# Fetching the experts' rows earlier, and the last two additions of a mixture-of-experts block in other pieces, on one Trainium2 core

## The chip, the cores and the metric

The kernel runs on one core of one Trainium2 chip. The metric is the device time of one launch in microseconds. The kernel before took 1689.24 us, the median of three runs (1687.09 to 1690.79).

## The reference

Four blocks run one after the other on x of 1024 tokens by 256 channels, all in float32: a gated delta rule attention, a perceptron, an attention with 4 heads and a mixture of experts. Only the last is touched here. Cut to what matters:

```python
xf = layernorm(x)
x_ = w_norm * (xf * rsqrt(mean(xf * xf) + EPS))
probs = softmax(x_ @ w_router)                    # 32 experts
w_topk, sel = top_k(probs, 4)
buf[e, place] = x_[token]                         # up to 128 rows for each expert
g = einsum('ech,ehf->ecf', buf, w_gate)           # F = 176
u = einsum('ech,ehf->ecf', buf, w_up)
y = einsum('ecf,efh->ech', silu(g) * u, w_down)
out = zeros.at[token].add(y * weight)
sh = sigmoid(x_ @ w_shared_gate) * (silu(x_ @ sw_gate) * (x_ @ sw_up) @ sw_down)
return x + xf + out + sh
```

## The kernel before

The program is a row of blocks. At the end of a block all engines meet at a barrier, and within one each engine goes through its own list in order and waits on semaphores. The last part has three blocks: a layer norm, `route_and_share`, and `experts`.

`route_and_share` finds each token's four experts, and GpSimd writes each token's row (289 numbers: 256 channels, 32 weights, the token's number) to its places in the DRAM tensor `expert_rows` (called `buf` in the code) with 32 indirect DMAs (L1657; semaphore `s_scat`). Meanwhile TensorE computes the shared expert (L1555, L1568), and VectorE adds that to x (L1645), which is the last thing in the block.

`experts` goes through the 32 experts one by one. For expert e, SP loads its 128 rows into one of six tiles `be` (L1700) and its down weights into one of four tiles `wd` (L1705). TensorE transposes the rows (`flip`, L1748), VectorE copies the result to `bT` (L1797), TensorE makes gate and up (`hidden`, L1756), ScalarE and VectorE make `hh` (L1843, L1803), TensorE transposes it (`flip_hidden`, L1764), ScalarE copies it (L1849), TensorE multiplies by `wd` (`output`, L1773), VectorE computes the rows' destinations (`places`, L1809 and L1811) and weighs the output into `ys` (`y_out`, L1815), and GpSimd adds `ys` to a sum in DRAM by an indirect DMA that accumulates (L1737). This last step is called the scatter below. There are two such sums, `expert_sum0` for the even experts and `expert_sum1` for the odd ones. A scatter waits until the one before it into the same sum has landed (`s_summed`), and `places(e)` waits for the landing of scatter e-4, since `place` and `ys` have four buffers.

TensorE's list is software pipelined. What is called iteration i below is one turn of this loop:

```python
            for e in range(E + 1):
                if e + 2 < E:
                    flip(e + 2)
                if e + 1 < E:
                    hidden(e + 1)
                if e < E:
                    flip_hidden(e)
                if e >= 1:
                    output(e - 1)
```

SP's list alternates rows and weights for the same expert. Weights of e wait for output e-4 (`s_yb`). So the rows of e, which stand behind the weights of e-1, cannot leave before output e-5 is done, at the end of iteration e-4, and `flip(e)` is the first thing in iteration e-2.

At the end SP waits for both sums, loads each in two halves into `part` (L1719), VectorE adds the four pieces to x (L1835), and SP stores x in two halves (L1724).

## Time and profile before

| | |
|---|---|
| median of 3 runs | 1689.24 us |
| the profiled execution: its own time | 1689.97 us |
| the profiled execution: its span | 1687.5 us |
| route_and_share, from the first product to the last addition | about 1478 to 1556 us |
| experts, from its first load to the last scatter's landing | 1556.6 to 1674.3 us |
| last loads, additions and stores | 1674.3 to 1687.1 us |

The times of the trace count from the start of its span. "PE" is TensorE's matmul side and "PEld" its weight loads, "DVE" is VectorE, "ACT" ScalarE, "POOL" GpSimd, "SPq" an instruction on SP's queue. A row "PE psum_banks L1748 <- DMA moe_be" is idle time of PE that a landing ended.

### The profile page before, as it was taken

How to read it: one execution, taken by the hardware profiler on the slowest of the kernel's cores; microseconds unless marked ns; L12 is line 12 of the kernel's file. 1: busy time of each engine (PE TensorE's matmuls, PEld its weight loads, DVE VectorE, ACT ScalarE, POOL GpSimd, SP SyncE). 2: the span in 40 equal slices, each digit the busy share in tenths (PEclk: the TensorE clock that was granted, in tenths of full speed). 3: DMA queues.
4: the chain of work that ended last, by engine and by line, in shares of the span. 5: the costliest groups of instructions: out<-in, count | busy, mean ns of one | idle time of the engine just before them, and what ended most of it. 6: DMA issues, size and time to landing. Idle time of an engine off the chain costs nothing. (4 is left out here: it accounts for less than half of the span.)

```text
span 1687.5 us, 26280 instructions
## 1 busy us (share of the span) xinstructions
PE 1424.7 (84%) x9464; PEld 1006.2 (60%) x9464; DVE 1058.4 (63%) x2172; ACT 768.4 (46%) x1796; POOL 722.6 (43%) x1181
## 2 busy tenths in 40 slices
PE   1555989999999999999999999988777888699874
PEld 1333667676777676777767767776535455455553
DVE  2534777877878787778787877865322355541443
ACT  0232655656556556565565565664220355110110
POOL 0065374382563653734735637430000288234443
PEclk9977889999999999999999999999888899889997
DMA  8111111111111111111111111010081000112666
GB/s 203 47 29 42 30 33 36 36 33 37 27 40 35 33 36 36 39 36 24 37 36 32 42 30 38 24 20 13 7 327 32 1 1 1 56 46 76 135 136 136
DMA packets 127039, 86.70 MB, mean 51 GB/s; under 512 B 92290, under 2 KB 112982, under 8 KB 126144
## 3 DMA queue, kind: packets, MB, share of 16 engines
q1 hardware_dynamic: 120768, 76.50, 17.1%
q0 software_dynamic: 6144, 8.53, 3.0%
q8 instruction: 76, 1.25, 0.3%
q14 instruction: 51, 0.42, 0.1%
HBM read 61.65 MB, written 23.76 MB: 51 GB/s over the span
## 5 line engine op out<-in xcount | busy, mean ns | idle before, releaser
L614 PE MATMUL psum_banks<-main_hT,heads_w_in 128*128 128x512 f32 x512 | 261.9, 645 | 11.9 <-DMA heads_w_in<-in_w_in 8.1
L939 DVE SCALAR_TENSOR_TENSOR heads_y<-psum_banks,gdn_conv_w,heads_y 128x1021 f32<-128x1021 f32 (+2 forms) x192 | 245.1, 1278 | 37.2 <-ACT heads_y L809 35.2
L1118 POOL TENSOR_TENSOR heads_XT<-heads_XT,heads_tmp 128x126 f32<-128x126 f32 (+22 forms) x496 | 211.8, 427 | 38.8
L1108 POOL TENSOR_TENSOR heads_A<-heads_A,heads_cb 128x1024 f32<-128x1024 f32 x16 | 37.7, 2355 | 397.5 <-DVE heads_nd_t L992 381.0
L1115 POOL TENSOR_TENSOR heads_tmp<-heads_XT,heads_A 128x126 f32<-128x126 f32 (+22 forms) x496 | 180.9, 365 | 38.9
L614 PEld LDWEIGHTS psum_banks<-main_hT,heads_w_in 128*128 128x128 f32 x512 | 102.1, 207 | 108.0 <-issue 92.9
L1445 POOL TENSOR_SCALAR attn_prob<-attn_prob,attn_rtotal 128x1024 f32<-128x1024 f32 x32 | 90.7, 2846 | 149.4 <-DVE attn_rtotal L1412 149.4
L746 PE MATMUL psum_banks<-heads_w_o,heads_ogT 128*128 128x256 f32 x512 | 121.1, 386 | 2.9 <-ACT heads_ogT L875 1.0
L715 PE MATMUL psum_banks<-heads_w_z,main_hT 128*128 128x256 f32 x512 | 123.5, 384 | 0.0
L809 ACT ACTIVATE heads_y<-psum_banks,gdn_conv_w 128x1024 f32<-128x1024 f32 x64 | 71.3, 1115 | 102.8 <-PE psum_banks L614 100.8
L827 ACT ACTIVATE heads_O<-psum_banks,gdn_coef 128x128 f32<-128x128 f32 x224 | 69.8, 363 | 86.2 <-PE psum_banks L645 84.0
L834 ACT ACTIVATE heads_Dt<-heads_Dl,gdn_coef 128x128 f32<-128x128 f32 x224 | 77.3, 393 | 66.9 <-DVE heads_Dl L952 66.5
L746 PEld LDWEIGHTS psum_banks<-heads_w_o,heads_ogT 128*128 128x128 f32 x512 | 95.1, 193 | 19.9 <-issue 8.5
L715 PEld LDWEIGHTS psum_banks<-heads_w_z,main_hT 128*128 128x128 f32 x512 | 93.1, 192 | 11.2
L947 DVE SCALAR_TENSOR_TENSOR heads_X<-psum_banks,gdn_coef,heads_v_s 128x128 f32<-128x128 f32 x224 | 67.8, 344 | 50.9 <-PE psum_banks L643 50.8
L652 PE MATMUL psum_banks<-heads_X,heads_Uf 128*128 128x128 f32 x448 | 75.5, 292 | 21.5 <-DVE heads_X L947 21.5
L652 PEld LDWEIGHTS psum_banks<-heads_X,heads_Uf 128*128 128x128 f32 x448 | 62.5, 193 | 52.1 <-issue 31.2
L952 DVE COPY heads_Dl<-psum_banks 128x256 f32<-128x256 f32 x128 | 53.8, 420 | 63.3 <-PE psum_banks L652 62.8
L845 ACT ACTIVATE heads_junk<-heads_og 128x128 f32<-128x128 f32 x256 | 78.0, 305 | 33.9 <-DVE heads_og L978 29.5
L658 PE MATMUL psum_banks<-heads_Dl,heads_At 128*128 128x128 f32 x512 | 86.6, 293 | 3.8 <-DVE heads_Dl L952 3.8
L1737 POOL DMA_INDIRECT expert_sum<-moe_ys,moe_place x32 | 49.6, 1549 | 80.8 <-DVE moe_ys L1815 76.9
L1132 POOL TENSOR_TENSOR heads_rs<-heads_var,gdn_minus_half 128x16 f32<-128x16 f32 x16 | 46.4, 2901 | 86.5 <-DVE heads_var L1063 86.5
(249 smaller groups left out, 3115.8 us busy)
## 6 DMA issues: line engine op xcount, KB each, us to landing
main_w_gu<-in_w_gu SPq DMA_DIRECT2D x4, 2816.0 KB, 24.7
heads_w_in<-in_w_in SPq DMA_DIRECT2D x16, 512.0 KB, 3.5
heads_A<-kk_blocks SPq DMA_DIRECT2D x64, 128.0 KB, 2.7
moe_wd<-in_w_down SPq DMA_DIRECT2D x32, 176.0 KB
expert_rows<-main_zeros SPq DMA_DIRECT2D x1, 4624.0 KB, 29.1
moe_be<-expert_rows SPq DMA_DIRECT2D x32, 144.5 KB, 3.3
heads_w_z<-in_w_z SPq DMA_DIRECT2D x16, 256.0 KB, 2.7
heads_w_o<-in_w_o SPq DMA_DIRECT2D x16, 256.0 KB, 2.6
```

The costliest lines, as they stand in the source:

```text
L614: ins = pe.matmul(out[:, half * 512:(half + 1) * 512], w_in[:, kd_, j * P:(j + 1) * P], hT[:, kd_, half * 512:(half + 1) * 512], start=kd_ ...
L652: ins = pe.matmul(bank_a[:, e], Uf[old][:, e * C + c], rhs, start=True, stop=True)
L658: ins = pe.matmul(bank_b[:, e], At[old][:, c * HD + e], Dl[:, e], start=True, stop=True)
L715: ins = pe.matmul(flat(bank[b][:, 2 * j:2 * j + 2]), hT[:, k, c * P:(c + 1) * P], w_z[:, k], start=k == 0, stop=k == KD - 1)
L746: ins = pe.matmul(flat(bank[b][:, 2 * j:2 * j + 2]), ogT[:, c * HD + e], w_o[:, e], start=e == 0, stop=e == HD - 1)
L809: act.activation(y[j][:], out, ACT.Copy, scale=conv_w[:, head, j, 3:4]).then_inc(pair_base.sem, 1)
L834: ins = act.activation(Dt[:, e], Dl[:, e], ACT.Copy, scale=coef[:, TAIL, h - 1, i:i + 1])
L845: act.activation(junk[:], og[(h - 1) % 2][:, c * HD + e], ACT.Square, accum_out=ms[:, c * HD + e:c * HD + e + 1]).then_inc(sq_ready.sem, 1)
L939: dve.scalar_tensor_tensor(y[j][:, shift:T], src[:, 0:T - shift], conv_w[:, head, j, t:t + 1], y[j][:, shift:T], ALU.mult, ALU.add).then_i ...
L1115: pool.tensor_tensor(tmp[:, 0:n, 0:m], bc_last(XT[:, 0:n, j], m), bc_mid(A0[:, j, j + 1:BLK], n), ALU.mult).then_inc(solve_step.sem, 1)
L1118: pool.tensor_tensor(XT[:, 0:n, j + 1:BLK], XT[:, 0:n, j + 1:BLK], tmp[:, 0:n, 0:m], ALU.add).then_inc(solve_step.sem, 1)
L1445: pool.tensor_scalar(prob[p % 2][s][:], prob[p % 2][s][:], rtotal[:, n:n + 1], None, ALU.mult).then_inc(s_norm, 1)
```

## The change

SP loads the first four `wd` tiles at the start of `route_and_share` and the first six `be` tiles in that same block, once all 32 scatters into `expert_rows` have landed. For this `be`, `wd` and their semaphores are made outside `experts`. In `experts`, SP's turn e now loads the rows of e+2 (after `y_out` and `places` of e-4) and then the weights of e (after output e-4). At the end, `expert_sum0` is waited for and loaded by itself in two halves, then `expert_sum1` in four quarters; VectorE makes two additions of 1024 and four of 512 elements a partition, and SP stores four quarters. No computation is left out.

```diff
+QUARTERS = 4
...
+        def load_rows(sp, e):
+            sp.dma_start(be[e % UB][:], buf[e * CAP:(e + 1) * CAP]).then_inc(s_be[e % UB], 16)
+
+        def load_down(sp, e):
+            sp.dma_start(wd[e % UN][:], d["w_down"][e]).then_inc(s_wd[e % UN], 16)
...
     with nc.Block() as block:
+        @block.sync
+        def _(sp):
+            for e in range(UN):
+                load_down(sp, e)
+            sp.wait_ge(s_scat, 16 * N)
+            for e in range(UB):
+                load_rows(sp, e)
...
-            def load_rows(e):
-                if e >= UB:
-                    sp.wait_ge(s_ys, e - UB + 1)
-                    sp.wait_ge(s_place, e - UB + 1)
-                sp.dma_start(be[e % UB][:], buf[e * CAP:(e + 1) * CAP]).then_inc(s_be[e % UB], 16)
-
-            def load_down(e):
-                if e >= UN:
-                    sp.wait_ge(s_yb, e - UN + 1)
-                sp.dma_start(wd[e % UN][:], d["w_down"][e]).then_inc(s_wd[e % UN], 16)
-
-            for e in range(UN):
-                load_rows(e)
-            for e in range(UN):
-                load_down(e)
             for e in range(UN, E):
-                load_rows(e)
-                load_down(e)
-            for i in range(SUMS):
-                sp.wait_ge(s_summed[i], 16 * (E // SUMS))
+                ahead = e + UB - UN
+                if ahead < E:
+                    sp.wait_ge(s_ys, ahead - UB + 1)
+                    sp.wait_ge(s_place, ahead - UB + 1)
+                    load_rows(sp, ahead)
+                sp.wait_ge(s_yb, e - UN + 1)
+                load_down(sp, e)
+            sp.wait_ge(s_summed[0], 16 * (E // SUMS))
             for half in range(2):
-                for i in range(SUMS):
-                    rows = sums[i][half * HALFT * P:(half + 1) * HALFT * P].rearrange("(t p) n -> p t n", p=P)
-                    sp.dma_start(part[i][:, half * HALFT:(half + 1) * HALFT], rows).then_inc(s_part[2 * i + half], 16)
+                rows = sums[0][half * HALFT * P:(half + 1) * HALFT * P].rearrange("(t p) n -> p t n", p=P)
+                sp.dma_start(part[0][:, half * HALFT:(half + 1) * HALFT], rows).then_inc(s_part[half], 16)
+            sp.wait_ge(s_summed[1], 16 * (E // SUMS))
+            for i in range(QUARTERS):
+                rows = sums[1][i * QT * P:(i + 1) * QT * P].rearrange("(t p) n -> p t n", p=P)
+                sp.dma_start(part[1][:, i * QT:(i + 1) * QT], rows).then_inc(s_part[2 + i], 16)
             o = out.rearrange("a (t p) n -> p (a t) n", p=P)
-            for half in range(2):
-                sp.wait_ge(s_add, SUMS * (half + 1))
-                mine = slice(half * HALFT, (half + 1) * HALFT)
+            for i in range(QUARTERS):
+                sp.wait_ge(s_add, 2 + i + 1)
+                mine = slice(i * QT, (i + 1) * QT)
                 sp.dma_start(o[:, mine], x[:, mine]).then_inc(s_out, 16)
...
             for half in range(2):
-                mine = x[:, half * HALFT:(half + 1) * HALFT]
-                for i in range(SUMS):
-                    dve.wait_ge(s_part[2 * i + half], 16)
-                    if i:
-                        dve.wait_ge(s_add, SUMS * half + i)
-                    dve.tensor_tensor(mine, mine, part[i][:, half * HALFT:(half + 1) * HALFT], ALU.add).then_inc(s_add, 1)
+                mine = slice(half * HALFT, (half + 1) * HALFT)
+                dve.wait_ge(s_part[half], 16)
+                dve.tensor_tensor(x[:, mine], x[:, mine], part[0][:, mine], ALU.add).then_inc(s_add, 1)
+            for i in range(QUARTERS):
+                mine = slice(i * QT, (i + 1) * QT)
+                dve.wait_ge(s_part[2 + i], 16)
+                dve.wait_ge(s_add, i // 2 + 1)
+                dve.tensor_tensor(x[:, mine], x[:, mine], part[1][:, mine], ALU.add).then_inc(s_add, 1)
```

SP's list of the kernel before, from the start of the block `experts` (`moe_be` are the row tiles, `moe_wd` the weight tiles, with their buffer numbers):

```order
L1694 UNCONDITIONAL_BRANCH
L1700 DMA moe_be0<-expert_rows 128x289
L1700 DMA moe_be1<-expert_rows 128x289
L1700 DMA moe_be2<-expert_rows 128x289
L1700 DMA moe_be3<-expert_rows 128x289
L1705 DMA moe_wd0<-in_w_down 88x512
L1705 DMA moe_wd1<-in_w_down 88x512
L1705 DMA moe_wd2<-in_w_down 88x512
L1705 DMA moe_wd3<-in_w_down 88x512
L1700 DMA moe_be4<-expert_rows 128x289
L1705 DMA moe_wd0<-in_w_down 88x512
L1700 DMA moe_be5<-expert_rows 128x289
```

SP's list of the changed kernel in the same place; the branches L1542 and L1711 are the border between `route_and_share` and `experts`:

```order
L1487 DMA moe_wd3<-in_w_down 88x512
L1484 DMA moe_be0<-expert_rows 128x289
L1484 DMA moe_be1<-expert_rows 128x289
L1484 DMA moe_be2<-expert_rows 128x289
L1484 DMA moe_be3<-expert_rows 128x289
L1484 DMA moe_be4<-expert_rows 128x289
L1484 DMA moe_be5<-expert_rows 128x289
L1542 UNCONDITIONAL_BRANCH
L1711 UNCONDITIONAL_BRANCH
L1484 DMA moe_be0<-expert_rows 128x289
L1487 DMA moe_wd0<-in_w_down 88x512
L1484 DMA moe_be1<-expert_rows 128x289
```

All six row tiles are now asked for ahead of the border, and in `experts` the first pair is the rows of expert 6 and the weights of expert 4, where it was the weights of expert 4 and then the rows of expert 5.

The end of SP's list, before:

```order
L1719 DMA moe_part0<-expert_sum0 128x4x256
L1719 DMA moe_part1<-expert_sum1 128x4x256
L1719 DMA moe_part0<-expert_sum0 128x4x256
L1719 DMA moe_part1<-expert_sum1 128x4x256
L1724 DMA out<-main_x 128x4x256 x2
```

and in the changed kernel:

```order
L1487 DMA moe_wd2<-in_w_down 88x512
L1487 DMA moe_wd3<-in_w_down 88x512
L1724 DMA moe_part0<-expert_sum0 128x4x256 x2
L1728 DMA moe_part1<-expert_sum1 128x2x256 x4
L1733 DMA out<-main_x 128x2x256 x4
```

Both halves of the first sum are ahead of the second, which comes in four pieces, and the store has four pieces too.

## Rows read from the trace of the kernel before

**Rows 1.** The page: TensorE's busy time and share of the span.

```profile
PE   1424.7 (84%) x9464; PEld 1006.2 (60%) x9464; DVE 1058.4 (63%) x2172; ACT 768.4 (46%) x1796; POOL 722.6 (43%) x1181
```

**Rows 2.** Waits, 1556 to 1675 us: total, times, longest.

```profile
POOL expert_sum L1737 <- DVE moe_ys L1815: 76.9, 28, 26.8
PEld psum_banks L1748 <- DMA moe_be<-expert_rows: 27.1, 25, 3.4
```

**Rows 3.** Timeline, start of the experts: start, duration, engine, what, idle before.

```profile
1540.75 0.97 POOL L1657 DMA_INDIRECT expert_rows<-moe_rows,route_dest  x1 [0.30 <-issue]
...
1555.23 0.88 DVE L1645 SCALAR_TENSOR_TENSOR main_x<-psum_banks,route_gate,main_x 128x256 f32<-128x256 f32 x2 [5.09 <-PE psum_banks L1568]
...
1556.59 1.75 SPq L1700 DMA_DIRECT2D moe_be<-expert_rows  x4
...
1558.89 0.86 PE L1748 MATMUL psum_banks<-main_ident,moe_be 128*128 128x128 f32 x4 [3.70 <-DMA moe_be<-expert_rows]
...
1559.89 2.68 PE L1756 MATMUL psum_banks<-main_w_gu,moe_bT 128*128 128x352 f32 x4
```

**Rows 4.** Timeline: flips of experts 3 and 4, without a wait.

```profile
1564.48 0.38 PE L1748 MATMUL psum_banks<-main_ident,moe_be 128*128 128x128 f32 x2
...
1566.97 0.39 PE L1748 MATMUL psum_banks<-main_ident,moe_be 128*128 128x128 f32 x2
```

**Rows 5.** Timeline: one iteration's end, and the last flip.

```profile
1602.17 0.30 SPq L1705 DMA_DIRECT2D moe_wd<-in_w_down  x1
1602.17 0.48 DVE L1815 TENSOR_SCALAR moe_ys<-psum_banks,moe_be 128x256 f32<-128x256 f32 x1
1602.57 0.35 SPq L1700 DMA_DIRECT2D moe_be<-expert_rows  x1
...
1603.51 1.55 POOL L1737 DMA_INDIRECT expert_sum<-moe_ys,moe_place  x1 [1.54 <-DVE moe_ys L1815]
...
1659.64 0.44 PE L1748 MATMUL psum_banks<-main_ident,moe_be 128*128 128x128 f32 x2 [0.47 <-DMA moe_be<-expert_rows]
```

**Rows 6.** Timeline of POOL: the last three scatters.

```profile
1665.99 1.55 POOL L1737 DMA_INDIRECT expert_sum<-moe_ys,moe_place  x1 [0.72 <-DVE moe_place L1811]
1668.22 1.55 POOL L1737 DMA_INDIRECT expert_sum<-moe_ys,moe_place  x1 [0.68 <-issue]
1670.51 1.55 POOL L1737 DMA_INDIRECT expert_sum<-moe_ys,moe_place  x1 [0.75 <-DMA expert_sum<-moe_ys,moe_place]
```

**Rows 7.** Issue to landing: row loads, scatters, scatters of 1568.55 and 1651.32.

```profile
DMA to landing us min/median/max: 2.2/3.3/5.2
...
DMA to landing us min/median/max: 3.7/3.8/5.6
...
DMA to landing us min/median/max: 4.5/4.5/4.5
...
DMA to landing us min/median/max: 4.7/4.7/4.7
```

**Rows 8.** Stretches: busy PE, PEld, DVE, ACT, POOL; granted clock; DMA share; GB/s.

```profile
1566.00:1667.00 101.00, 83.38 (x363) 55.42 (x361) 46.08 (x154) 18.54 (x61) 45.92 (x30) 0.97 0.66 128
...
1560.00:1563.40 3.40, 3.40 (x8) 2.05 (x9) 0.67 (x3) 0.32 (x1) 0.00 (x0) 0.50 0.73 234
```

**Rows 9.** The chain that ended last: start, duration, what.

```profile
1670.51 3.75 DMA expert_sum<-moe_ys,moe_place
...
1675.85 7.05 DMA moe_part<-expert_sum
...
1682.93 1.23 DVE main_x L1835
```

**Rows 10.** DMA issues: count, size of each, median issue to landing.

```profile
heads_w_z<-in_w_z SPq DMA_DIRECT2D x16, 256.0 KB, 2.7
...
out<-main_x SPq DMA_DIRECT2D x2, 512.0 KB, 3.0
```

**Rows 11.** Stretch of the last loads and stores, columns as in Rows 8.

```profile
1675.00:1687.50 12.50, 0.00 (x0) 0.00 (x0) 4.90 (x4) 0.00 (x0) 0.00 (x0) 0.50 0.79 252
```

More of the change, by code:

```diff
@@ L1475, in mixture @@
         loaded = {n: a.sem(f"{n}_loaded") for n in names + ["sw_gu", "sw_down"]}
+        be = [a.sb(f"be{i}", [P, XW]) for i in range(UB)]
+        wd = [a.sb(f"wd{i}", [FH, 2, D]) for i in range(UN)]
+        s_be = [a.sem(f"rows{i}_loaded") for i in range(UB)]
+        s_wd = [a.sem(f"wd{i}_loaded") for i in range(UN)]
+        def load_rows(sp, e):
+            sp.dma_start(be[e % UB][:], buf[e * CAP:(e + 1) * CAP]).then_inc(s_be[e % UB], 16)
+        def load_down(sp, e):
+            sp.dma_start(wd[e % UN][:], d["w_down"][e]).then_inc(s_wd[e % UN], 16)
         route_stack = ExitStack()
@@ L1492, in mixture, with route_and_share @@
         with route_stack:
-            route_and_share(nc, b, x, hT, consts, rows, w_r, iota, token, loaded, sw_gu, sw_down, buf, s_zeroed)
-        experts(nc, a, x, consts, d, w_gu, gu_loaded, spare, loaded["spare"], buf, sums, s_sums, out)
-def route_and_share(nc, a, x, hT, consts, rows, w_r, iota, token, loaded, sw_gu, sw_down, buf, s_zeroed):
+            route_and_share(nc, b, x, hT, consts, rows, w_r, iota, token, loaded, sw_gu, sw_down, buf, s_zeroed, load_rows, load_down)
+        experts(nc, a, x, consts, w_gu, gu_loaded, spare, loaded["spare"], sums, s_sums, out, be, wd, s_be, s_wd, load_rows, load_down)
+def route_and_share(nc, a, x, hT, consts, rows, w_r, iota, token, loaded, sw_gu, sw_down, buf, s_zeroed, load_rows, load_down):
     N = NT * TOPK
@@ L1664, with experts @@
 UB = 6
-def experts(nc, a, x, consts, d, w_gu, gu_loaded, spare, spare_loaded, buf, sums, s_sums, out):
+def experts(nc, a, x, consts, w_gu, gu_loaded, spare, spare_loaded, sums, s_sums, out, be, wd, s_be, s_wd, load_rows, load_down):
     ident = consts["ident"]
-    be = [a.sb(f"be{i}", [P, XW]) for i in range(UB)]
-    wd = [a.sb(f"wd{i}", [FH, 2, D]) for i in range(UN)]
     bT = [a.sb(f"bT{i}", [P, KD, P]) for i in range(UN)]
@@ L1683, in experts @@
     yb = [a.psum([P, 512]) for i in range(2)]
-    s_be = [a.sem(f"rows{i}_loaded") for i in range(UB)]
-    s_wd = [a.sem(f"wd{i}_loaded") for i in range(UN)]
     s_tb, s_bt, s_gb, s_sg, s_hh = (a.sem(n) for n in ("rows_flipped", "rowsT_written", "hidden_ready", "silu_written", "hidden_written"))
@@ L1689, in experts @@
     s_empty, s_place = a.sem("empty_rows_found"), a.sem("places_ready")
-    s_part, s_add, s_out = [a.sem(f"part{i}_loaded") for i in range(2 * SUMS)], a.sem("part_added"), a.sem("out_written")
-    HALFT = NT // 2
+    s_part, s_add, s_out = [a.sem(f"part{i}_loaded") for i in range(2 + QUARTERS)], a.sem("part_added"), a.sem("out_written")
+    HALFT, QT = NT // 2, NT // QUARTERS
     with nc.Block() as block:
@@ L1720, in _ @@
             o = out.rearrange("a (t p) n -> p (a t) n", p=P)
-            for half in range(2):
-                sp.wait_ge(s_add, SUMS * (half + 1))
-                mine = slice(half * HALFT, (half + 1) * HALFT)
+            for i in range(QUARTERS):
+                sp.wait_ge(s_add, 2 + i + 1)
+                mine = slice(i * QT, (i + 1) * QT)
                 sp.dma_start(o[:, mine], x[:, mine]).then_inc(s_out, 16)
-            sp.wait_ge(s_out, 32)
+            sp.wait_ge(s_out, 16 * QUARTERS)
```

## The prediction

> **What bounds the kernel now.** I read the page first, for the share of each engine: TensorE is busy 84% of the span [rows 1]. That is an average over four blocks, and the change touches only the last 130 us, so I went on to the waits of that stretch. The reader is to see two rows there [rows 2]. GpSimd's long wait for `ys` is idle time of an engine with little to do. TensorE's wait for the landing of expert rows is another matter: 27.1 us in 25 waits on its weight-load side, on the engine that all others wait for. The stage is bound by the latency of the row loads, not by TensorE's work.
>
> The timeline says by how much. Expert 4's flip follows expert 3's without a wait, 1566.97 - 1564.48 = 2.49 us later [rows 4]. That is TensorE's own time for one iteration. From expert 4's flip to the last flip, that of expert 31 at 1659.64 [rows 4, 5], are 27 iterations in 92.67 us, 3.43 us each. The rest, 0.94 us an iteration, is waiting for rows, and what follows from it.
>
> Why do rows come late? SP issues weights at the end of iteration e-4 and the rows of e 0.40 us behind them (1602.17, 1602.57) [rows 5], and the load takes 3.3 us in the median [rows 7]. Only iteration e-3 lies between. 0.40 + 3.3 = 3.7 us against 2.49 us of work cannot be hidden.
>
> **The change, part by part.** The predicted sum is made against the profiled execution, 1689.97 us with a span of 1687.5, so 2.47 us lie outside the span and stay. Its difference is then taken from the median of 1689.24; the two are 0.04% apart.
>
> *First loads moved up.* VectorE's last addition ends at 1555.23 + 0.88 = 1556.11, SP issues 0.48 us later, and the first flip starts at 1558.89 [rows 3]. With the rows in place it can start about when SP's first instruction did, say 1556.7: 2.2 us less. What hides the moved loads is the shared expert's last products: the last scatter into `expert_rows` starts at 1540.75 [rows 3]. Were it as slow as the slowest scatter of the next block, 5.6 us [rows 7], and then six issues at 0.44 us each (1.75 for four [rows 3]), all would be issued by 1549. Seven microseconds of cover are left. Were it gone, this 2.2 us would be too. SP has nothing else to do in that block; the four weight loads at its start pass no queue in which others stand. The clock comes on top: TensorE stands still for 3.70 us there [rows 3], and then has a stretch at half clock, 1560 to 1563.4, where the granted clock is 0.50, that is 1.2 of 2.4 GHz [rows 8]; the first `hidden` takes 2.68 us [rows 3]. At full clock the same work takes half of these 3.4 us, so without the dip 1.7 us more would go. After the change TensorE still stands still for about 1.5 us. No row shows what that does, so the bounds are 2.2 and 3.9 us, and I take 3.0.
>
> *Rows two experts further ahead.* The rows of e now wait for `y_out(e-6)`, which ends 0.48 us into iteration e-4 [rows 5]; so two whole iterations less 0.5 us lie before their use, 4.5 us at 2.49 us each, against a landing of 3.3 us in the median and 5.2 at most [rows 7], and rows go ahead of the weights, not behind them. Nearly all of the waiting for rows should go. The weights are put 0.9 us later than before, and are used three iterations after, so that costs nothing.
>
> What is late next? Two things could be. TensorE is the floor, 2.49 us. The other is the scatter. GpSimd takes 1.55 us for one and starts the next at best 2.23 to 2.29 us after (1665.99, 1668.22, 1670.51) [rows 6]: below 2.49. But a scatter also waits for the one before last. The one of 1665.99 was down by about 1669.8 and the next into that sum started at 1670.51, so the chain costs (landing + 0.76)/2 for each expert: 2.28 us at a landing of 3.8 [rows 7]. This holds only while landings stay short. I went through all 32. Six flips in the loop found their rows in place (the first at 1566.97, the others at 1586.55, 1614.22, 1624.16, 1640.15 and 1649.78), and the scatters in just these six iterations took 4.5, 4.7, 5.2, 4.8, 5.6 and 4.7 us, on average 4.9 (first, last and longest in [rows 7]); the other 26 took 3.7 to 4.1. Loads and scatter collide when iterations are short, and after the change all are short. At 4.9 us the chain costs 2.83 us an expert.
>
> So the period lies between 2.49 and 2.83. A scatter that is held back starts the next but one later, and so falls further behind the loads of its own iteration, which should part them again; no row shows this. I take 2.65: 27 x (3.43 - 2.65) = 21.1 us. Bounds: 25.4 us and 16.2 us.
>
> The DMA engines are busy 0.66 of 1566 to 1667 [rows 8], that is 0.66 x 3.43 = 2.3 us for each expert. At 2.65 us this is 0.85, so they don't yet bound, but there is little room. The Trainium skill (DMA: Bandwidth & Descriptors, "Issuing engines are not separate DMA queues") says that DMAs of all issuing engines end up on the same 16 engines and interleave, which is a rule against this change; the six slow scatters agree with it. If one read it so that every scatter costs 4.9 us, the term would be the lower bound.
>
> *A backlog of scatters.* With the chain this near the period, GpSimd will be behind when the loop ends, and the end waits for it: from nothing to four buffers' worth. I take 1.5 us lost, bounds 0 and 4.
>
> *The end.* The first sum's last scatter lands 1670.51 - 1668.22 = 2.29 us ahead of the second's [rows 6], and its loads leave by that much earlier. The loads now run one after the other until 1675.85 + 7.05 = 1682.90 [rows 9]; half of them starts 2.29 us sooner, so the last one lands up to 2.29 us sooner. The last addition is 512 elements wide, half of 1.23 us [rows 9]: 0.6 less. The last store is of 256 KB; the nearest row of that size took 2.7 us against 3.0 for 512 KB [rows 10]: 0.3 less. Against this, three quarters and not one half are stored while loads still run, on engines that are busy 0.79 of this stretch [rows 11]; I take 0.3 us for it. Sum 2.9 us; bounds 1.0 (the DMA engines are full and only the end of the row is shorter) and 3.4. More issues (ten for six) cost nothing, since SP's 0.4 us each are shorter than the transfers.
>
> The Trainium skill (DMA: Bandwidth & Descriptors, "Anatomy of one DMA") gives a DMA 2.0 us plus its bytes over 436 GB/s, and its rule is to batch. By that an estimate for a 256 KB store is 2.6 us against 3.2 for 512 KB, so the end would gain 0.3 us more than by the rows.
>
> *Sum.* 3.0 + 21.1 - 1.5 + 2.9 = 25.5 us. 1689.97 - 25.5 = 1664.5 for the profiled execution, 1663.7 from the median; I say 1664.
>
> **The rivals.**
>
> 1. TensorE bounds the loop outright. For it: its 2.49 us are more than the chain's 2.28. Against: the six slow scatters. 3.9 + 25.4 + 3.4 = 32.7 us: 1656.5. I count everything with a period up to 2.75 as one case with my forecast (it runs from 1656 to 1667), chance 0.60, of which 0.15 for this end.
>
> 2. The scatter chain becomes the bound, at 2.83 us or more. For it: all six short iterations had slow landings, without exception, and `places` hands the delay on to VectorE, from there to SP's row loads and to TensorE. Against: they were slow beside loads that left in a different order. 16.2 + 3.0 + 2.9 - 3 = 19.1 us: 1670. Chance 0.27.
>
> 3. Rows still come late, since their landing grows with the load. For it: 5.2 us was seen [rows 7]. With 5.2 in each, two iterations last 0.5 + 5.2 us, 2.85 each: 27 x 0.58 = 15.7, with the other terms 15.7 + 3.0 - 1.5 + 2.9 = 20.1: 1669. Against: rows now leave ahead of the weights. Chance 0.07.
>
> 4. Slower than before. The mechanism is again the scatter chain, with a landing so long that it takes back start and end too: the period would have to pass 3.43 + (3.0 + 2.9)/27 = 3.65 us, so a landing of 2 x 3.65 - 0.76 = 6.5 us in every scatter, where the largest of 32 is 5.6 [rows 7]. At 7.0 us the period is 3.88 and the sum -12.2 + 5.9 - 3 = -9: 1698. Chance 0.03.
>
> 5. The change doesn't do what it says: the early rows come no earlier, or another wait of TensorE (for `bT`, `hh`, `ys`) takes the place of the one for rows. VectorE is busy 46.08 of 101 us [rows 8], 1.6 us for each iteration of 3.43 and so less than 2.49, ScalarE far less, and the early loads have seven microseconds of cover. If it were so, the end's 2.9 us would stay: 1686, which is 0.17%. Chance 0.03.
>
> **How the numbers follow.** The time is that of the likeliest case, 1664. Its own range is 1656 to 1667. Case 2 and case 3 reach to about 1672, so the range 1655 to 1672 leaves out cases 4 and 5 and the far end of case 2: some 0.15 in all. About 0.2% (3.4 us) is what a measurement of this kernel can tell from no change. The forecast and cases 1 to 3 are all faster, 0.94; within 0.2% is case 5, 0.03; slower is case 4, 0.03.
>
> **What would show it.** In the profile of the changed kernel: the waits of PE and PEld for `moe_be` fall from 27.1 us to under 5; the first flip starts within 1 us of the last addition, and the clock dip at the start is short or gone; flips come 2.5 to 2.75 us apart; GpSimd waits for `expert_sum` landings where it waited for `ys`, and the median landing of scatters is above 4 us; DMA share in the loop is 0.8 or more; the last `part` load lands about 6.4 us after the last scatter, where it was 8.6. The prediction is wrong if scatters land in 3.8 us or above 5 us throughout, since the period, which carries four fifths of the sum, hangs on that; or if TensorE waits for something not named here.

## The result, and the profile after

| | before | changed |
|---|---|---|
| median | 1690.01 us (4 runs, 1687.09 to 1695.97) | 1668.59 us (4 runs, 1666.66 to 1671.7) |
| profiled execution: time, span | 1689.97, 1687.5 us | 1669.73, 1667.4 us |
| end of the last addition of `route_and_share` to the end of the span | 131.4 us | 106.3 us |

The changed kernel takes 0.9874 of the time of before, with a 95% interval of 0.9854 to 0.9893: 21.4 us less. The forecast was 1664 with a range of 1655 to 1672.

I read the waits first, as before [rows 2], here from 1540 to 1660 us. Columns: us in total, times, longest.

```profile
POOL expert_sum L1746 <- DVE moe_ys L1824: 42.4, 10, 34.3
POOL expert_sum L1746 <- DVE moe_place L1820: 21.1, 17, 2.9
DVE moe_empty L1818 <- DMA expert_sum<-moe_ys,moe_place: 18.6, 17, 1.9
POOL expert_sum L1746 <- DMA expert_sum<-moe_ys,moe_place: 5.3, 3, 2.3
PEld psum_banks L1757 <- DMA moe_be<-expert_rows: 1.9, 3, 1.1
PE psum_banks L1757 <- PEq L1542: 1.7, 1, 1.7
PE psum_banks L1757 <- DMA moe_be<-expert_rows: 0.7, 1, 0.7
```

TensorE's weight-load side waits 1.9 us for rows where it waited 27.1. What is late now is the scatter: VectorE's `places` (L1818) waits for scatters to land 17 times, and GpSimd waits for `places` 17 times. GpSimd's wait looks like one for VectorE, but VectorE is itself waiting for GpSimd's earlier scatter; the two rows are one circle.

The timeline of TensorE, for the start of the experts and the last flips [rows 3 to 5]:

```profile
1554.72 5.50 PE L1589 MATMUL psum_banks<-route_sw_down,route_hsh 128*128 128x256 f32 x22
1561.91 0.63 PE L1757 MATMUL psum_banks<-main_ident,moe_be 128*128 128x128 f32 x4 [1.69 <-PEq L1542]
1562.90 1.45 PE L1765 MATMUL psum_banks<-main_w_gu,moe_bT 128*128 128x352 f32 x4 [0.37 <-DVE moe_bT L1806]
...
1568.30 0.38 PE L1757 MATMUL psum_banks<-main_ident,moe_be 128*128 128x128 f32 x2
...
1629.52 0.44 PE L1757 MATMUL psum_banks<-main_ident,moe_be 128*128 128x128 f32 x2 [0.74 <-DMA moe_be<-expert_rows]
...
1637.04 0.38 PE L1757 MATMUL psum_banks<-main_ident,moe_be 128*128 128x128 f32 x2
```

The first flip waits for TensorE's own queue, not for rows, and starts 0.78 us after the last addition (1561.13). Expert 4's flip is at 1568.30 and expert 31's at 1637.04: 27 iterations in 68.74 us, 2.55 us each. TensorE runs at its own pace.

The table by stretches; columns: stretch, its length, busy time and count of PE, PEld, DVE, ACT and POOL, granted clock, DMA share, GB/s.

```profile
1472.28:1561.13 88.85, 79.19 (x240) 44.11 (x240) 22.05 (x62) 10.08 (x16) 31.41 (x32) 0.91 0.20 67
1561.13:1568.30 7.17, 6.03 (x29) 4.21 (x29) 2.60 (x9) 1.51 (x5) 0.00 (x0) 1.00 0.00 0
1568.30:1637.04 68.74, 67.92 (x325) 49.50 (x324) 38.21 (x134) 16.23 (x54) 38.30 (x25) 1.00 0.81 170
```

The granted clock is 1.00 (2.4 GHz) from the first flip on; the dip of before [rows 8] is gone. The DMA engines are busy 0.81 of the loop. The first row is `route_and_share`: 88.85 us. The same block of the kernel before, in its first profile:

```profile
1478.40:1556.11 77.71, 76.68 (x240) 43.56 (x240) 22.15 (x62) 10.20 (x16) 31.49 (x32) 0.94 0.16 56
```

11.1 us more, in code in which the change only adds SP's loads. 8.6 us of it are idle time of TensorE (9.7 for 1.0), the rest is the same 240 products taking longer (79.19 us at a granted clock of 0.91, for 76.68 at 0.94). Experiments 1, 2, 4, 5 and 9 to 12 are about this.

The chain that ended last, from the scatter of expert 13 on (start, us, what):

```profile
1606.66 4.59 DMA expert_sum<-moe_ys,moe_place
1611.30 0.49 issue
1612.00 4.85 DMA expert_sum<-moe_ys,moe_place
1616.91 0.49 issue
1617.61 4.49 DMA expert_sum<-moe_ys,moe_place
...
1633.87 4.84 DMA expert_sum<-moe_ys,moe_place
1638.76 0.49 issue
1639.46 3.75 DMA expert_sum<-moe_ys,moe_place
...
1653.07 5.08 DMA expert_sum<-moe_ys,moe_place
1658.16 0.36 SPq L1728
1658.57 0.47 SPq L1728
1659.08 4.23 DMA moe_part<-expert_sum
1663.34 0.70 DVE main_x L1846
```

Scatter follows scatter into the same sum: 1612.00 - 1606.66 = 5.34 us for two experts, 5.61 for the next two. It is a chain through memory, 0.76 us longer than each landing, and it is slower than TensorE's 2.49. So a backlog grows in the four buffers: the last scatter starts 1653.07 - 1637.04 = 16.03 us after the last flip, where it was 1670.51 - 1659.64 = 10.87 [rows 5, 6]. Once SP has no more experts to load (its last weights leave by 1637.5), landings fall to 3.75.

The delay reaches SP too. SP waits for `places` before it loads rows into the tile that this frees, and GpSimd waits for the same `places` with its scatter. So, once scatters are late, the two leave together. Timelines of GpSimd and SP:

```profile
1612.00 1.54 POOL L1746 DMA_INDIRECT expert_sum<-moe_ys,moe_place  x1 [1.09 <-DVE moe_place L1820]
...
1612.10 0.33 SPq L1484 DMA_DIRECT2D moe_be<-expert_rows  x1
```

There it stops: rows are fetched two experts ahead, and the flips of this stretch are 2.49 to 2.56 us apart.

The end, SP's and VectorE's timeline [rows 9, 10]:

```profile
1654.18 0.95 SPq L1724 DMA_DIRECT2D moe_part<-expert_sum  x2
1658.16 1.90 SPq L1728 DMA_DIRECT2D moe_part<-expert_sum  x4
1662.15 3.00 SPq L1733 DMA_DIRECT2D out<-main_x  x4
```

The first sum is fetched 4 us ahead of the second. The last scatter landed at 1658.15, and the span ends 9.25 us later, where it was 13.24. But that last landing took 5.08 us, with the loads of the first sum beside it, where it took 3.75 before. The two have to be taken together: from the start of the last scatter to the end of the span are 14.31 us, where there were 1687.5 - 1670.51 = 16.99, so 2.7 us less.

The stretch from the last addition to the end adds up: start 3.7 (2.00 to the first flip, 1.69 to expert 4's flip), loop 23.9, backlog -5.2, end 2.7 (4.0 after the last landing, less 1.3 for that landing itself), together 25.1 us = 131.4 - 106.3. The spans differ by 20.1, because of what lies ahead of this stretch: `route_and_share` 11.1 us longer, and the work ahead of it, which the change doesn't touch, 6.1 us shorter in this execution.

### The profile page after: what moved, and what is told of

It is laid out like the page before. It is cut to its first block and busy times, and to the rows that moved or that the text cites. A ratio compares the mean times of both kernels' runs of the same rounds, so it can differ in the third digit from the quotient of the medians.

```text
span 1667.4 us, 26287 instructions
## 1 busy us (share of the span) xinstructions
PE 1416.1 (85%) x9464; PEld 1004.9 (60%) x9464; DVE 1055.0 (63%) x2174; ACT 767.7 (46%) x1796; POOL 721.7 (43%) x1181
## 5 line engine op out<-in xcount | busy, mean ns | idle before, releaser
L643 PE MATMUL psum_banks<-gdn_S,heads_kT 128*128 128x256 f32 x224 | 71.3, 400 | 11.3 <-DVE gdn_S L960 9.6
```

The lines of the kernel that those rows point to most:

```text
L643: pe.matmul(flat(bank_a[:, 0:2]), kT[(h - 1) % 3][:, cs], flat(S[:]), start=True, stop=True).then_inc(a_full.sem, 1)
```

## The experiments

Each row gives the length of `route_and_share` (first product to end of the last addition), the stretch from there to the end of the span, the mean distance of the last 27 flips, and the time from the last flip to the start of the last scatter.

| | median us | ratio to before, 95% interval | route | rest | flips | backlog |
|---|---|---|---|---|---|---|
| before, first profile | 1690.0 | | 77.7 | 131.4 | 3.43 | 10.9 |
| changed, first profile | 1668.6 | 0.9854 to 0.9893 | 88.9 | 106.3 | 2.55 | 16.0 |
| changed again | 1663.1 | 0.9832 to 0.9873 | 87.5 | 106.8 | 2.51 | 16.1 |
| ahead only | 1674.9 | 0.9906 to 0.9936 | 88.1 | 112.5 | 2.52 | 16.3 |
| early only | 1685.4 | 0.9963 to 0.9987 | 88.2 | 122.9 | 3.25 | 10.8 |
| tail only | 1687.6 | 0.9975 to 1.0011 | 89.6 | 126.2 | 3.30 | 10.8 |
| before again | 1695.4 (one run) | | 90.7 | 126.7 | 3.24 | 10.9 |
| four sums | 1663.7 | 0.9825 to 0.9869 | 90.8 | 101.0 | 2.49 | 10.0 |
| no weight loads | 1663.4 | 0.9824 to 0.9867 | 89.2 | 102.1 | 2.49 | 10.8 |
| three sums | 1665.9 | 0.9828 to 0.9879 | 90.8 | 103.3 | 2.50 | 10.0 |
| half the scatters | 1657.7 | 0.9765 to 0.9833 | 77.7 | 106.0 | 2.53 | 16.1 |
| paced scatters | 1660.2 | 0.9802 to 0.9857 | 77.5 | 109.0 | 2.54 | 16.1 |
| paced, three sums | 1654.3 | 0.9769 to 0.9819 | 77.5 | 104.4 | 2.49 | 10.0 |
| before, paced | 1675.2 | 0.9886 to 0.9933 | 77.7 | 129.3 | 3.34 | 10.9 |

The stages of an edited kernel are better set beside "before again" than beside the first profile of before. That one is alone twice: its `route_and_share` is short, and its flips are 3.43 us apart, where the four other profiles with the old order of loads have 3.24 to 3.34. Over 27 flips this is 5 us, so "rest" is 126.7 in "before again" and not 131.4.

**1. The changed kernel again.** No edit.

> The changed kernel once more, nothing edited. In its first profile route_and_share took 88.9 us from its first product (1472.28) to the end of its last addition (1561.13), against 77.7 us before, since ScalarE and VectorE started several shared-expert instructions 7 us late. Theory A: this comes from SP's new work in that block; the profile shows about 88 us again. Theory B: it is an accident of one execution; the profile shows 77 to 78 us, and a time 8 to 11 us below that profile's 1669.7, about 1660, with other runs in between. In both theories the flips are 2.5 to 2.6 us apart, scatter landings have a median of 4.4 us or more, and the last scatter starts 4 to 6 us after the last y_out.

Measured 1663.05 us (1659.71 to 1668.77), ratio 0.9853. The experts stage repeats within half a microsecond, 106.8 for 106.3, and so does the long `route_and_share`, 87.5. It is no accident of one execution. The expectation put this down to SP's new work in that block; experiment 2 refutes that.

**2. Rows further ahead, alone.** The early block of SP and the new end are taken out; the loop keeps the change.

```diff
-        @block.sync
-        def _(sp):
-            for e in range(UN):
-                load_down(sp, e)
-            sp.wait_ge(s_scat, 16 * N)
-            for e in range(UB):
-                load_rows(sp, e)
```

> Only the rows two experts further ahead; first loads and end as before. Theory 1 (GpSimd's scatter chain bounds the loop once rows are early): the loop's flips come 2.5 to 2.6 us apart, from flip 4 to the last landing it takes 16 to 19 us less than before, 1671 to 1674 in all. Rival (the early loads and the end carry much of the gain): above 1678. Theory A on the route block (SP's work there delays it): route_and_share takes 77 to 78 us here, for SP is idle in it.

Measured 1674.86, ratio 0.9921: some 13 us, the largest part of the whole, 0.9 us above what was expected. The rest of the span is 112.5 us against 131.4, or 126.7 in the profile of before again. The first flip comes 2.84 us after the last addition, as before; flips are 2.52 apart, the backlog is the full 16.3. `route_and_share` is 88.1 us long here too, with SP idle in it, so the early loads don't lengthen it.

**3. Early rows and weights, alone.** The loop and the end of before, with the early block.

```diff
-                ahead = e + UB - UN
-                if ahead < E:
-                    sp.wait_ge(s_ys, ahead - UB + 1)
-                    sp.wait_ge(s_place, ahead - UB + 1)
-                    load_rows(sp, ahead)
+                if e >= UB:
+                    sp.wait_ge(s_ys, e - UB + 1)
+                    sp.wait_ge(s_place, e - UB + 1)
+                    load_rows(sp, e)
```

> Only the first four weight tiles and six row tiles loaded in route_and_share; in the loop SP's order is that of before, and so is the end. The start should gain 2.2 to 3.9 us. Theory A (SP's work delays the block by 11 us): 7 to 9 us slower than before, about 1698, and the block takes 88 us. Theory B (accident): 1686 to 1688, and the block 77 to 78 us. In both the loop is unchanged, 3.4 us an expert.

Measured 1685.42, ratio 0.9975. The first flip comes 0.81 us after the last addition; the flips stay 3.25 apart, and TensorE waits for rows as it did (27.1 us before):

```profile
PEld psum_banks L1754 <- DMA moe_be<-expert_rows: 25.2, 25, 2.3
```

The expectation tied a block of 88 us to a time of 1698 and a time of 1686 to a block of 77. The run has the block of the one, 88.2, and the time of the other. What both had wrong is the block of the kernel before, which experiment 5 shows.

**4. The new end, alone.** Before, with the two sums fetched and added as in the changed kernel.

```diff
-            for i in range(SUMS):
-                sp.wait_ge(s_summed[i], 16 * (E // SUMS))
+            sp.wait_ge(s_summed[0], 16 * (E // SUMS))
...
+            sp.wait_ge(s_summed[1], 16 * (E // SUMS))
+            for i in range(QUARTERS):
```

> Only the end: first sum loaded as soon as it is complete, last addition and store in pieces of 512. By the prediction 2.9 us less, bounds 1.0 and 3.4: 1687. If the early loads slow the last scatter (5.08 us to landing in the changed kernel's profile against 3.75 before), 1.3 us of that is taken back and the last scatter lands in about 5 us here too: 1.6 to 2 us less, 1688.

Measured 1687.6, ratio 0.9993 with 1 inside its interval: by its time alone no effect can be told. The stage is plain all the same. From the start of the last scatter to the end of the span are 14.29 us, where before has 1687.5 - 1670.51 = 16.99: 2.7 us less. In the timeline of SP:

```profile
1672.81 0.99 SPq L1720 DMA_DIRECT2D moe_part<-expert_sum  x2
1675.12 1.90 SPq L1724 DMA_DIRECT2D moe_part<-expert_sum  x4
```

The last scatter started at 1671.31 and SP's second row at 1675.12, 3.8 us later: here the last scatter landed as fast as before, with the first sum's loads 1.5 us behind its start (1.1 in the changed kernel). Yet the 14.29 us are those of the changed kernel, 14.31, so the slow last landing there is no loss; presumably the loads that slow it are done the earlier. Experiment 9 has a last landing of 3.9 us and 14.4 us to the end. The block `route_and_share` is that of before, unchanged, and took 89.6 us.

**5. Before again.** No edit.

> The kernel before once more, nothing edited, for its profile. In the four kernels run so far route_and_share took 87 to 90 us in the profile, also where that block's code is untouched (only the end edited: 89.6 us), against 77.7 us in the first profile of before. Theory C (most executions have the 7 us late starts of ScalarE and VectorE in this block, and the first profile of before was one without): 87 to 90 us here. Theory D (where tiles and semaphores are allocated, which all edited kernels changed, brings the stall): 77 to 78 us here.

Measured one execution of 1695.4 us; block and flips are what is read here, not the time. ScalarE's timeline in `route_and_share`, and the block's row in the table by stretches:

```profile
1516.31 0.60 ACT L1583 ACTIVATE route_up<-psum_banks 128x512 f32<-128x512 f32 x1 [2.84 <-DVE route_hsh L1592]
1524.80 0.60 ACT L1583 ACTIVATE route_up<-psum_banks 128x512 f32<-128x512 f32 x1 [7.89 <-remote]
1540.21 0.60 ACT L1583 ACTIVATE route_up<-psum_banks 128x512 f32<-128x512 f32 x1 [14.82 <-issue]
```

```profile
1475.47:1566.16 90.69, 83.28 (x240) 46.19 (x240) 22.07 (x62) 10.21 (x16) 31.47 (x32) 0.87 0.14 48
```

The long block is in the kernel before as well; its first profile was the exception. ScalarE starts 7.89 and then 14.82 us after it was free, where its turn is 2.84. A comparison of the two first profiles by their spans hides 11 us. The flips here are 3.24 us apart, so the loop of before is 5 us shorter in this profile than in its first.

**6. Four sums.** Scatters go to four sums in turn, so each waits for the fourth before it; only two are loaded and added, so the output leaves out half of the experts' contributions.

```diff
-SUMS = 2
+SUMS = 4
...
-                    dve.wait_ge(s_summed[e % SUMS], 16 * ((e - UN) // SUMS + 1))
+                    dve.wait_ge(s_summed[(e - UN) % SUMS], 16 * ((e - UN) // SUMS + 1))
```

> The changed kernel with four sums in DRAM for the scatters, of which only two are loaded and added at the end, so the output lacks half of the experts. A scatter waits for the fourth before it. Theory 1 (the chain through two sums bounds the scatters, 2.66 us an expert): they follow each other at 2.5 us or less, the last starts 10.9 us after the last flip as before and not 16.1, and the time falls by 4 to 6 us to 1657 to 1659. Rival (the DMA engines themselves are full, so that scatters land later the more are in flight): landings rise to 6 us or more and the time falls by less than 2 us.

Measured 1663.68, ratio 0.9847. The waits for landings are gone; GpSimd's only large wait is this:

```profile
POOL expert_sum L1750 <- DVE moe_ys L1828: 63.9, 29, 37.6
```

The last scatter starts 10.0 us after the last flip in place of 16.0. The two-sum chain was the whole backlog. The 1657 to 1659 us expected were missed: the profiled stage is 5.3 us shorter (101.0 for 106.3), but the time is not told apart from the changed kernel's (0.9832 to 0.9873 and 0.9854 to 0.9893).

**7. No weight loads in the loop.** Experts 4 to 31 use the down weights of the first four, so the output is that of other weights.

```diff
-                sp.wait_ge(s_yb, e - UN + 1)
-                load_down(sp, e)
...
-                pe.wait_ge(s_wd[e % UN], 16 * (e // UN + 1))
+                pe.wait_ge(s_wd[e % UN], 16)
```

> The changed kernel without the weight loads in the loop, so that experts 4 to 31 use the first four experts' down weights. 176 KB an expert less to move. Theory 1 says that scatters land late because loads collide with them: the median landing falls from about 4.7 us to 3.8 to 4.1, the chain to 2.3 to 2.45 us an expert, below the flips' 2.49, and 4 to 6 us go, 1657 to 1659. Rival (scatters land late because they come more often, whatever is loaded): landings stay above 4.5 us and the time within 2 us.

Measured 1663.43, ratio 0.9845. The chain still goes through scatters, but they are faster:

```profile
1602.48 4.56 DMA expert_sum<-moe_ys,moe_place
1607.79 4.54 DMA expert_sum<-moe_ys,moe_place
1613.08 4.16 DMA expert_sum<-moe_ys,moe_place
...
1637.93 3.79 DMA expert_sum<-moe_ys,moe_place
1642.48 3.73 DMA expert_sum<-moe_ys,moe_place
```

The ten in the chain take 3.73 to 4.56 us; all 32 have a median of 3.8, against 4.7 in the changed kernel (both estimates from the ends of their packets, which lie 0.34 us ahead of the landing where the trace has both). Scatters start 2.47 us apart, closer than in the changed kernel, so it is not their own rate that slows them, and the backlog is 10.8. Most of what makes scatters slow is the weight loads beside them; the row loads alone leave some slow. By the stage 4.2 us are gained (102.1 for 106.3), but the median misses the 1657 to 1659 us expected and is not told apart from the changed kernel's. The Trainium skill (DMA: Bandwidth & Descriptors, "Issuing engines are not separate DMA queues") says that DMAs of all engines interleave on the same 16 engines, and this run agrees: taking away SP's transfers shortens GpSimd's by 0.9 us.

**8. Three sums, all added.** As experiment 6, with three sums, all loaded and added; the third is zeroed ahead of the routing block, and nothing is left out.

```diff
-SUMS = 2
+SUMS = 3
...
+            for k, i in enumerate((2, 0)):
+                sp.wait_ge(s_summed[i], 16 * len(range(i, E, SUMS)))
...
+            sp.wait_ge(s_summed[1], 16 * len(range(1, E, SUMS)))
```

> The changed kernel with three sums, all three added, the third zeroed at the start of the mixture. Theory 1: the scatters keep up with the flips, 2.5 us an expert, which gives back 5 us; the third sum's 1 MB costs about 4 us of transfer, of which over half lies under the last scatters: 1660 to 1662, 1 to 3 us faster than the changed kernel. Rival (the end is bound by bytes): 1663 to 1666, no gain.

Measured 1665.86 (1659.17 to 1671.98), ratio 0.9854: the rival's time, no gain that the time shows. The backlog is 10.0 us, 6.0 less. But the end is longer, as SP's timeline shows:

```profile
1652.68 3.23 SPq L1727 DMA_DIRECT2D moe_part<-expert_sum  x4
1659.94 1.90 SPq L1731 DMA_DIRECT2D moe_part<-expert_sum  x4
1664.67 2.20 SPq L1736 DMA_DIRECT2D out<-main_x  x4
```

The last scatter started at 1652.60 with four loads of 512 KB issued right beside it, and was down only at 1659.94, 7.3 us later. Half of the gain goes there: from the last flip to the end of the span are 27.3 us, against 30.4.

**9. Half the scatters in the routing block.** Sixteen of 32 are left out, so two of each token's four experts get no row and their contributions are missing. The waits for their landings are halved to match.

```diff
+                    if s >= 2:
+                        continue
```

> The changed kernel with 16 of the 32 scatters of token rows in the routing block left out (each token's last two experts get no row, so the output lacks their contributions; the loop over experts does the same work on the buffers). The question is the stall of about 11 us in the routing block of every profile but the first one of the kernel before (88 to 91 us in place of 77.7). Theory S: VectorE and ScalarE are held back by GpSimd's scatters: with 16 the scatters end about 20 us earlier, before the engines' late starts, and the block takes 77 to 80 us; the whole about 1656 to 1660 (10 us less). Rival F: the late starts have nothing to do with the scatters (something that comes 40 us into the block whatever else runs): the block stays at 87 to 91 us, the time within 2 us of the changed kernel's 1665 to 1669. Loop over experts as in the changed kernel by both: flips 2.5 apart.

Measured 1657.66, ratio 0.9799. `route_and_share` takes 77.73 us, as in the one profile without the stall:

```profile
1472.77:1550.50 77.73, 76.70 (x240) 43.57 (x240) 22.15 (x62) 10.20 (x16) 15.84 (x16) 0.94 0.15 49
```

The scatters (last start 1514.6) are over at about the time at which the late starts begin in the other profiles. Its own trace has the beginning of them: one start of VectorE 0.4 us late (1515.83) and one of ScalarE 0.9 (1517.91), and none after. The stall hangs on GpSimd's scatters.

**10. Paced scatters.** All 32, each waiting for the landing of the one two before it; nothing left out.

```diff
+                    if n >= 2:
+                        pool.wait_ge(s_scat[n % 2], 16 * (n // 2))
...
-                                            oob_is_err=False).then_inc(s_scat, 16)
+                                            oob_is_err=False).then_inc(s_scat[n % 2], 16)
```

> The changed kernel with the 32 scatters of the routing block let out two at a time (each waits for the landing of the one two before it); complete output. Theory S1 (held back by many scatters in flight at once): no late starts, a block of 77 to 80 us, the time 7 to 10 us less, as long as the paced scatters (16 pairs by some 3 us: 48 us from 1495, so to about 1543) end before the block does. Theory S2 (held back for as long as any scatters run): the late starts end with the last scatter, which comes up to 8 us later: block 90 to 98 us, time 0 to 8 us more. Rival F (no link with scatters): block 87 to 91 us, time unchanged within 2 us.

Measured 1660.17, ratio 0.9829. The block is 77.47 us long, with 32 scatters in it:

```profile
1469.30:1546.77 77.47, 76.44 (x240) 43.42 (x240) 22.16 (x62) 10.20 (x16) 31.36 (x32) 0.94 0.20 68
```

The last scatter starts at 1542.50. So 32 scatters, going on for longer than before (51 us for 40), need not bring the stall. How many are under way at once differs little: one lands after about 2.5 us, in the first profile of before as here, and they start 1.28 us apart there and 1.65 here. Whether the rate decides, or the wait itself, these runs don't separate. The pacing has a price: rows are loaded only once the last has landed, and the cover of the early loads is used up. TensorE's first flip is 1.7 us after the last addition in place of 0.8, with a granted clock of 0.50 (1.2 GHz) from 1550.4 to 1553.4 us behind it, and the rest of the span is 109.0 us for 106.3.

**11. Paced scatters and three sums.** Edits 8 and 10 together, nothing left out.

> The two edits together that helped: the routing block's scatters let out two at a time and three sums in turn (complete output). If the two gains are of separate stages they add up: block 77.5 us (measured with pacing alone), last scatter 10.0 us after the last flip (measured with three sums), end after the last scatter 17.3 us in place of 14.5; by the stage lengths 3 us less than with pacing alone, so 1655 to 1659 beside 1660.2, and a stretch from the last addition to the end of about 103 to 106. Rival: the third sum's later landing and its added part loads take back what the shorter backlog gives, and the time is the 1660 of pacing alone (1659 to 1663).

Measured 1654.29 (1651.84 to 1659.28), ratio 0.9794. Block 77.5, backlog 10.0, rest of the span 104.4: both gains are there, and the rest is shorter than 109.0 - 3.0 = 106.0, which the two alone would give. The time is just below the 1655 to 1659 expected. The interval lies below the changed kernel's; against pacing alone (0.9802 to 0.9857) they overlap, so that the third sum helps is shown by the stage and not by the time. It is the fastest version found with nothing left out.

**12. Before, paced.**

> The kernel before with the paced scatters alone. Theory S: the stall is common to before and after, and the first profile of before merely escaped it, so that pacing gives both about the same: block 77 to 79 us, 1690 - 8 = 1680 to 1684. With it the change itself is worth 20 to 24 us against a base that has no stall either (1660.2 of the paced changed kernel). Rival: before mostly runs without the stall (as in its first profile), and pacing leaves it at 1688 to 1692, the change then being worth about 30 us with pacing and 22 without.

Measured 1675.19 (1673.3 to 1681.55), ratio 0.9909, 5 us less than the 1680 to 1684 expected. Block 77.73. Before was slowed by the stall too, and pacing alone gives it 15 us by the ratio and 13.5 by the medians on this chip (1688.66 for the kernel before), about two thirds of what the change gives. This also answers a doubt about experiments 9 to 12: they ran on two chips of which no profile with all 32 scatters unpaced exists, but on both the kernel before took what it takes elsewhere (1689.68 and 1688.66), so it is not that the stall is missing there. With both paced the change is worth 0.9829 / 0.9909 = 0.9919, 13.6 us with some 6 us of uncertainty from the two intervals (15.0 by the two medians), where 20 to 24 were expected and the two profiles' rests differ by 129.3 - 109.0 = 20.3. The profiled execution of the paced kernel before was the slowest of its six. Why the others are up to 8 us faster stays open; no trace of them exists.

## Why the prediction was right

**What bounds it.** Right. With rows two experts ahead the waits for rows fall from 27.1 to 1.9 us, and this part alone makes more than half of the difference (experiment 2, and experiment 3 the other way round).

**First loads moved up: 3.0 us forecast, 3.7 measured** in the profile, within its bounds of 2.2 and 3.9. The first flip starts 0.78 us after the last addition and the clock does not dip. The cover held in every run but the paced ones, where its end is seen.

**The period: 2.65 us forecast, 2.55 measured; a term of 21.1 that was 23.9.** The mechanism ahead of it was right: with all iterations short, scatters land in 4.5 to 4.9 us on the chain, and the chain costs (landing + 0.76)/2. What was mis-sized is how far that reaches. The period was set between TensorE's 2.49 and the chain's 2.83, as if part of the chain's pace came through to the flips; rival 2 has the path: "`places` hands the delay on to VectorE, from there to SP's row loads and to TensorE". It does reach VectorE (17 waits) and SP's row loads, but not TensorE. The four buffers between TensorE and the scatter, and rows two experts ahead, take up the difference until the loop is over (scatters start 2.68 us apart, from 1569.88 to 1653.07, flips 2.55); TensorE's weight loads wait for rows three times in all, 1.9 us.

**A backlog: -1.5 us forecast, -5.2 measured.** This is the same difference of paces, booked at the end. Its bound of 4 was too small. I had split one quantity, the pace of the scatters, into two terms as if they were independent; over loop and backlog together the forecast was 19.6 and the trace has 18.8. Experiments 6 and 8 show that the backlog is that of the chain: with more sums the last scatter is 10.0 us behind the last flip, less than before the change.

**The end: 2.9 us forecast; 2.7 by experiment 4, and 4.0 - 1.3 = 2.7 in the changed kernel.** Right, though with another make-up. The last `part` load lands 5.2 us after the last scatter, not 6.4, and that scatter takes 1.3 us longer: the forecast had a collision of stores with loads and none of the first sum's loads with the last scatter. The 256 KB stores took 2.4 us in the median; the estimate of 2.6 us from the Trainium skill (DMA: Bandwidth & Descriptors, "Anatomy of one DMA") is near this, though the fit there is for DMAs issued from GpSimd, and these are issued by SP.

**The sum: 25.5 us forecast, 25.1 in the stage.** Two sizes were off, by 2.8 and 3.7 us, and nearly cancelled. That the sum agrees so closely is luck in one more way: it is made against the first profile of before, whose flips are 3.43 us apart. Against the second, with 3.24, the stage gives 126.7 - 106.3 = 20.4 us. The medians differ by 21.4, and in the second comparison the ratio makes it 24.8 (the two medians alone 27.0); executions of one kernel spread over 9 us and more, and the time cannot say more.

**What was missing.** The prediction took `route_and_share` as fixed. It has a stall of 10 to 13 us that the first profile of before did not show, and that all nine other profiles with the 32 scatters unpaced did. Both kernels have it, so the comparison of medians stands, though with both paced the change comes out at 13.6 us and not 20, which stays unexplained. A change worth two thirds of this one was lying there.

**The rivals.** TensorE as the bound (1656.5) came nearest for the loop: flips are at its pace. The scatter chain as the bound (1670) was right on what runs on the path that ends last, and its time is nearer to the first median, 1668.6, than the forecast's 1664 is, and further from the second, 1663.1. Both were at work, one for the loop and one for its end. Late rows, slower, and no effect did not occur.

## What to carry to other kernels

Buffers between a fast and a slow stage need not remove the slow stage's cost; here they moved it to the end of the loop. Count it once, as (iterations) x (difference of paces), here 31 x (2.68 - 2.49) = 5.9 us for a backlog that grew by 5.2, and look for it after the last iteration. When latency of one stream is hidden, look for a chain through memory (here an addition into the same sum) and for what the new pace does to its transfers. And profile the unchanged kernel twice before subtracting spans: in the two profiles of before one stage is 13 us longer and another 5 us shorter.

## What was unexpected of the hardware

GpSimd issued its 32 scatters of `route_and_share` 1.28 us apart without a wait. ScalarE and VectorE then started work late whose inputs the timeline shows as computed: the timeline of the changed kernel has

```profile
1513.16 0.60 ACT L1604 ACTIVATE route_up<-psum_banks 128x512 f32<-128x512 f32 x1 [2.89 <-PE psum_banks L1576]
1523.70 0.60 ACT L1604 ACTIVATE route_up<-psum_banks 128x512 f32<-128x512 f32 x1 [9.94 <-remote]
1539.81 1.07 ACT L1604 ACTIVATE route_up<-psum_banks 128x512 f32<-128x512 f32 x2 [15.51 <-remote]
```

and the last late starts come a few us after the last scatter (which starts at 1534.6). TensorE, which takes its turns with the two, is idle for 9.7 us of the block (88.85 - 79.19). Shown: it goes away with half the scatters (experiment 9) and with all of them two at a time (10 to 12), it does not need SP's loads (2) or the change (4, 5), and the first profile of before escaped it with the same scatters at the same pace. The trace also says what came late. Its record of semaphore updates has, in the profile of before again, an update of the semaphore that VectorE waits for at 1520.56 and one at 1530.39; the TensorE products that it waits for are over at 1517.98 and 1521.42 by the timeline. VectorE starts 0.09 us after the update both times, as it does in undisturbed turns. ScalarE starts 0.02 us after its update at 1524.77, whose product was over at 1519.70. So the waiting engines were not slow to start: TensorE's signal was late, by 2.6 to 9 us in these three (ends of products are modelled, but in undisturbed turns the update is within 0.02 us of them).

Not shown: why. One more thing differs between the profiles. Of the 512 semaphore updates by which the 32 scatters tell of their landing, the first profile of before has all and the paced ones 457 and more, while the nine with the stall have 119 to 212. Experiment 9, hardly stalled, has 90 of 256, so the two don't always go together. The recording of the execution may have a part in the stall, or the updates may be what is too many; the runs don't tell, and the record doesn't say how executions without a kept trace were recorded. That pacing shortens the median of the kernel before by 13.5 us is measured either way.

Two loads of 512 KB issued 1.0 to 1.1 us behind a scatter made its landing 5.1, 5.4 and 5.6 us for 3.75 (experiments 1 and 10 and the first profile), and four right beside it 7.3 and 7.4 (8 and 11); 1.5 us behind it, it landed in 3.8 and 3.9 (4 and 9). Fetching the first result early can delay the last one. Here that cost nothing: with two loads, the end came 14.3 to 14.5 us after the last scatter's start in all five.
